# Three-pass embedding in rounded parts, router columns inside other products, and a new order of a turn

## The reference

```python
h = patches @ W.T + b            # 196 patches of 768 pixels -> 192
h = concat([cls, h]) + pos_embed
h = concat([h, txt], axis=1)     # (32, 274, 192)
h = h + attention(layernorm(h))  # 12 heads of 16, rotary q and k, causal
n = layernorm(h)
pc = softmax(n @ Wsc + bsc); pu = softmax(n @ Wsu + bsu)    # two routers, 4 experts each
common = expert[argmax(pc)](n)   # 192 -> 768 -> gelu -> 192
unique = expert_u[argmax(pu)](n) # counts only for tokens past the capacity 2192 of their common expert
out = h + common + dropped * unique
```

## Time and profile before

| | |
|---|---|
| median of 3 runs | 1303.76 us (1300.44 to 1304.24) |
| the profiled execution, own time | 1305.39 us |
| its span, first to last instruction | 1303.5 us |
| mean granted TensorE clock | 0.962 |
| TensorE / VectorE / ScalarE / GpSimd busy | 92% / 68% / 43% / 48% |

### The profile page before, as it was taken

How to read it: one execution, slowest core, us unless ns; L and a number is a source line. 1 busy time by engine, 2 the same in 40 slices (tenths; PEclk the granted TensorE clock), 3 DMA queues, 4 the chain that set the end, 5 groups by cost and what they waited for, 6 DMA issues and landing times.

```text
span 1303.5 us, 33182 instructions
## 1 busy us (share of the span) xinstructions
PE 1202.0 (92%) x12718; PEld 1026.7 (79%) x12718; DVE 883.1 (68%) x1979; ACT 555.9 (43%) x959; POOL 621.8 (48%) x990
## 2 busy tenths in 40 slices
PE   5799999999999999999999999884899999999993
PEld 4667777777777877877787777674899999999993
DVE  5667677777777778678777767745898755554441
ACT  1134434444434443434443444332454555555540
POOL 4133333334543553454444544443552677765665
PEclk8899999999999999999999999885899999999997
DMA  6001121122312322232232222237787688987651
GB/s 204 31 30 42 44 75 45 43 63 84 108 56 61 115 93 58 84 125 62 82 99 89 80 75 67 66 108 271 272 271 253 208 276 270 293 261 255 220 186 32
DMA packets 84367, 168.03 MB, mean 129 GB/s; under 512 B 16446, under 2 KB 57701, under 8 KB 84208
## 3 DMA queue, kind: packets, MB, share of 16 engines
q1 hardware_dynamic: 70544, 139.88, 33.7%
q0 software_dynamic: 13664, 26.00, 5.6%
HBM read 123.83 MB, written 45.45 MB: 130 GB/s over the span
## 4 chain that ended last, share of the span: by engine, by line
PE 46%; DVE 22%; issue 12%; POOL 12%; DMA 3%; ACT 2%; SPq 1%; POOLq 0%; DVEq 0%; ACTq 0%
PE h_ps L1677 10%; PE y_ps L1688 9%; DVE capped L995 4%; POOL sorted_d L235 4%; PE round_banks L591 3%; PE gen L553 3%; PE gen L511 3%; POOL PT L877 3%; DVE xn L1011 3%; PE round_banks L564 3%; PE gen L520 2%; DVE nm L999 2%; DVE nm L997 2%; POOL rstd L870 2%; PE round_banks L578 2%
## 5 line engine op out<-in xcount | busy, mean ns | idle before, releaser
L760 ACT ACTIVATE PT<-round_banks 128x1752 f32<-128x1752 f32 x96 | 156.6, 1631 | 175.4 <-PE round_banks L591 175.4
L877 POOL TENSOR_SCALAR_AFFINE_SELECT PT<-PT 128x512 f32<-128x512 f32 x192 | 117.8, 637 | 206.3 <-ACT PT L760 205.8
L1767 ACT ACTIVATE Gl<-h_ps,W 128x256 f32<-128x256 f32 x264 | 115.8, 474 | 172.1 <-PE h_ps L1677 163.9
L1688 PE MATMUL y_ps<-W,Gl 128*128 128x192 f32 x1056 | 181.2, 325 | 0.0
L1688 PEld LDWEIGHTS y_ps<-W,Gl 128*128 128x128 f32 x1056 | 171.3, 189 | 0.0
L1677 PE MATMUL h_ps<-XH,Wh 128*128 128x256 f32 x528 | 149.0, 299 | 7.0 <-DVE Wl L1834 2.8
L511 PE MATMUL gen<-w_emb,xT 128*128 128x192 f32 (+1 forms) x768 | 143.8, 339 | 7.8 <-DMA ident<-in_ident_dram 7.8
L1677 PE MATMUL h_ps<-XH,Wl 128*128 128x256 f32 x528 | 141.4, 289 | 0.0
L511 PEld LDWEIGHTS gen<-w_emb,xT 128*128 128x128 f32 (+1 forms) x768 | 119.6, 171 | 16.7 <-DMA ident<-in_ident_dram 7.8
L591 PEld LDWEIGHTS round_banks<-QKT 32*128 32x128 f32 x2304 | 95.3, 187 | 46.7 <-DVE nm L997 23.0
L995 DVE TENSOR_TENSOR capped<-round_banks,masks_f 128x1024 f32<-128x1024 f32 x96 | 116.2, 1211 | 17.3 <-PE round_banks L564 16.8
(11 more groups left out here) (273 smaller groups left out, 2448.4 us busy)
## 6 DMA issues: line engine op xcount, KB each, us to landing
W<-in_experts_dram SPq DMA_DIRECT2D x44, 771.0 KB, 5.3
W<-in_experts_dram SPq DMA_DIRECT2D x44, 672.0 KB
xT<-in_xT_dram SPq DMA_DIRECT2D x32, 591.0 KB, 4.4
X<-sorted_d SPq DMA_DIRECT2D x35, 386.0 KB, 6.2
stage<-rows_d SPq DMA_DIRECT2D x64, 192.0 KB
rows_d<-h SPq DMA_DIRECT2D x32, 192.0 KB
out_dram<-h SPq DMA_DIRECT2D x32, 192.0 KB
rows_d<-xn SPq DMA_DIRECT2D x32, 192.0 KB
```

What stands on the lines that cost most here:

```text
L760: act.activation(PT[(JG * b + j) % 2][:], R[:, :, 0:438], ACT.Exp, scale=SCALE).then_inc(exps, 1)
L877: pool.affine_select(x[:, :, at:at + P], x[:, :, at:at + P], [[0, GH], [1, P]], ALU.is_ge, 0.0, base=0, channel_multiplier=-1)
L1688: mm = pe.matmul(y_ps[t.par][:, k * D:(k + 1) * D], Gl[t.par][:, f, k * P:(k + 1) * P], W[t.i][:, W2O + f * D:W2O + (f + 1) * D], start=(f ...
L1767: act.activation(Gl[t.par][:, f, :], h_ps[f % 3][:, 0:ROWS], ACT.Gelu, bias=W[t.i][:, B1O + f:B1O + f + 1]).then_inc(g_ready, 1)
```

## The change

It has four parts.

1. **Embedding in rounded parts.** Pixels x are split into `xh`, rounded to the format fp32r by ScalarE (`round_pixels`), and `xl` = x - `xh` by GpSimd (`rest_of_pixels`); the weights likewise, once at the start. A chunk is then one product of `xh` with both weight parts side by side (384 columns) and one of `xl` with the high part (192 columns). VectorE adds the two halves of the bank. Both splits of image t + 1 stand at the end of turn t on their engines.
2. **Router as extra columns.** The router is linear in h, and h is the embedding plus the attention's output. Eight columns are added to the value weights and to the output weights (`DE` = 200); the part from V is scaled by the standard deviation and kept (`part_logits`), that from WO is added, and the sum is scaled with `rstd2` and given its bias in `soften`. The centred router weights and their product with the output weights are made in turns 0 to 2 with R's banks. X2, RT, X2t and RTt, with their copies, go.
3. **Second normalisation on ScalarE.** `normalise` does scale and shift of `xn2` by one activation per tile; GpSimd makes the shift (`shift`). The tail's stays on VectorE.
4. **New order of a turn.** TensorE: M0, values 1, values 2, X, S0, V0, QK0, M1, E0, V1, S1, QK1, UT0, UT1, M2, E1, AT, T, values 0, KQ0, KQ1, MT, S2, KQ2, WO. VectorE and ScalarE follow; GpSimd's root for LN1 comes behind both rotary additions.

```diff
-STEADY = [("PV1", 4), ("PV2", 4), ("E0", 0), ("X", 1), ("E1", 0), ("V0", 1), ("QK0", 1), ("UT0", 4), ("UT1", 4), ("QK1", 1),
-          ("KQt0", "1"), ("KQt1", "1"), ("X2", 5), ("V1", 1), ("PV0", 3), ("XTt", "0"), ("ATt", "8"), ("RTt", "10"), ("UTt", "7"),
-          ("AT", 4), ("RT", 5), ("RK", "12"), ("QKt", "0"), ("X2t", "9"), ("KQ0", 1), ("KQ1", 1), ("MT", 2), ("Vt", "0"), ("KQ2", 1), ("WO", 4),
-          ("WOt", "8")]
+STEADY = [("PV1", 4), ("PV2", 4), ("X", 1), ("V0", 1), ("QK0", 1), ("E0", 0), ("V1", 1), ("QK1", 1), ("UT0", 4), ("UT1", 4),
+          ("KQt0", "1"), ("KQt1", "1"), ("E1", 0), ("AT", 4), ("XTt", "0"), ("ATt", "8"), ("UTt", "7"), ("PV0", 3),
+          ("QKt", "0"), ("KQ0", 1), ("KQ1", 1), ("RK", "12"), ("MT", 2), ("Vt", "0"), ("KQ2", 1), ("WO", 4), ("WOt", "8")]
...
-        w_emb = sb("w_emb", [P, EC, D])
-        w_qkv = sb("w_qkv", [P, 2, 3 * D])
-        w_o = sb("w_o", [P, 2, D])
+        w_emb = sb("w_emb", [P, EC, 2, D], F32R)
+        w_qkv = sb("w_qkv", [P, 2, 3 * D + NE])
+        w_o = sb("w_o", [P, 2, DE])
         w_r = sb("w_r", [P, 2, NE])
+        r_bias = sb("r_bias", [P, NE])
+        woT = sb("woT", [KC, 2, 2, KC + 1])
         minus_half = sb("minus_half", [P, 2])
 
         xT = [sb(f"xT{i}", [P, EC, NPATCH + 1]) for i in range(2)]
+        xh = sb("xh", [P, EC, NPATCH + 1], F32R)
+        xl = sb("xl", [P, EC, NPATCH + 1], F32R)
...
             def embed(b, k):
                 if k == 0:
-                    pe.wait_ge(x_in[b % 2], 16 * (b // 2 + 1))
+                    if b == 0:
+                        pe.wait_ge(emb_low, 1)
+                    pe.wait_ge(xl_set, b + 1)
                 g = fill(f"E{k}", b)
                 cols, m = (slice(0, P), P) if k == 0 else (slice(P, NPATCH + 1), IMG1)
                 for c in range(EC):
-                    mm = pe.matmul(g[0:m, 0:D], xT[b % 2][:, c, cols], w_emb[:, c, :], start=(c == 0), stop=(c == EC - 1))
+                    if c:
+                        pe.matmul(g[0:m, 0:D], xl[:, c, cols], w_emb[:, c, 0, :], start=False, stop=False, skip_group_check=True)
+                    mm = pe.matmul(g[0:m, 0:2 * D], xh[:, c, cols], w_emb[:, c, :, :].rearrange("p s d -> p (s d)"),
+                                   start=(c == 0), stop=(c == EC - 1), skip_group_check=True)
+                    if c == 0:
+                        pe.matmul(g[0:m, 0:D], xl[:, c, cols], w_emb[:, c, 0, :], start=False, stop=False, skip_group_check=True)
                 filled(f"E{k}", b, mm)
...
-            def route(use, i, xTs, tiles):
-                g = fill(use, i)
-                for k in range(tiles):
-                    o = g[:, k * NE:(k + 1) * NE]
-                    pe.matmul(o, xTs[:, 0, tok(k)], w_r[0:KC + 1, 0, :], start=True, stop=False)
-                    mm = pe.matmul(o, xTs[0:KC, 1, tok(k)], w_r[0:KC, 1, :], start=False, stop=True)
-                filled(use, i, mm)
+            def centre_router():
+
+                pe.wait_ge(consts_set, n_set)
+                pe.matmul(R[0:KC, 0, 0:NE], K.ones[0:KC, 0:KC], w_r[0:KC, 0, :], start=True, stop=False)
+                pe.matmul(R[0:KC, 0, 0:NE], K.ones[0:KC, 0:KC], w_r[0:KC, 1, :], start=False, stop=True).then_inc(mean_filled, 1)
+
+            def turn_output_weights():
+
+                pe.wait_ge(later_in, 16 * len(later))
+                for j in range(2):
+                    for c in range(2):
+                        at = (2 * j + c) * (KC + 1)
+                        mm = pe.transpose(R[0:KC, 1, at:at + KC + 1], w_o[0:KC + 1, c, j * KC:(j + 1) * KC], ident[0:KC + 1, 0:KC + 1])
+                mm.then_inc(wo_turned, 1)
+
+            def mix_output_weights():
+
+                pe.wait_ge(wo_copied, 1)
+                pe.wait_ge(centred, 1)
+                for c in range(2):
+                    o = R[0:KC + 1, 2, c * NE:(c + 1) * NE]
+                    pe.matmul(o, woT[:, 0, c, :], w_qkv[0:KC, 0, 3 * D:3 * D + NE], start=True, stop=False)
+                    mm = pe.matmul(o, woT[:, 1, c, :], w_qkv[0:KC, 1, 3 * D:3 * D + NE], start=False, stop=True)
+                mm.then_inc(wo_mixed, 1)
+                pe.wait_ge(wo_set, 1)
...
+            def round_pixels(b):
+
+                act.wait_ge(x_in[b % 2], 16 * (b // 2 + 1))
+                if b:
+                    act.wait_ge(g_filled[bank("E1", b - 1)], nth("E1", b - 1))
+                act.activation(xh[:], xT[b % 2][:], ACT.Copy).then_inc(xh_set, 1)
+
+            act.wait_ge(first_in, 16 * len(first))
+            act.activation(w_emb[:, :, 0, :], w_raw, ACT.Copy).then_inc(emb_high, 1)
+            round_pixels(0)
             act.wait_ge(consts_set, n_set)
...
             def copy_values(use, i, k):
                 g = take(use, i)
-                emptied(use, i, act.activation(V[i % 4][:, k, :, 0:HD], g[:, 0:D].rearrange("p (h d) -> p h d", d=HD), ACT.Copy))
+                act.activation(V[i % 4][:, k, :, 0:HD], g[:, 0:D].rearrange("p (h d) -> p h d", d=HD), ACT.Copy)
+                act.wait_ge(std_ready, i + 1)
+                emptied(use, i, act.activation(part[:, i % 8, k, :], g[:, D:DE], ACT.Copy, scale=std[:, i % 2, k:k + 1]))
+
+            def normalise(b):
+
+                if b >= 2:
+                    act.wait_ge(rows_out[b % 2], stored(b - 2))
+                act.wait_ge(shift2_ready, b + 1)
+                c = UNIT * (b // 4) + 2 * (b % 4)
+                for k in range(2):
+                    ins = act.activation(xn2[b % 2][:, k, :], h[b % 8][:, k, :], ACT.Identity,
+                                         bias=shift2[:, b % 2, k:k + 1], scale=rstd2[:, c + k:c + k + 1])
+                ins.then_inc(xn2_ready, 1)
...
                     copy_heads(t.pre, 2)
+                if t.t + 1 < B:
+                    round_pixels(t.t + 1)
...
+            def rest_of_pixels(b):
+
+                pool.wait_ge(xh_set, b + 1)
+                if b:
+                    pool.wait_ge(g_filled[bank("E1", b - 1)], nth("E1", b - 1))
+                pool.tensor_tensor(xl[:], xT[b % 2][:], xh[:], ALU.subtract).then_inc(xl_set, 1)
+
             for x in (rr, rrt, nm, *ht, *QKT):
                 pool.memset(x[:], 0.0).then_inc(zeroed, 1)
+            rest_of_pixels(0)
...
+            def shift(b):
+
+                c = UNIT * (b // 4) + 2 * (b % 4)
+                if b:
+                    pool.wait_ge(shift2_ready, b)
+                pool.tensor_scalar(minus[:], mv[:, LN2, :, 0], -1.0, None, ALU.mult).then_inc(minus_ready, 1)
+                pool.wait_ge(rstd_ready[LN2], b + 1)
+                pool.wait_ge(minus_ready, b + 1)
+                if b >= 2:
+                    pool.wait_ge(xn2_ready, b - 1)
+                pool.tensor_tensor(shift2[:, b % 2, :], minus[:], rstd2[:, c:c + 2], ALU.mult).then_inc(shift2_ready, 1)
+
+            def spread(b):
+
+                pool.wait_ge(rstd_ready[LN1], b + 1)
+                if b >= 2:
+                    pool.wait_ge(g_emptied[bank("V1", b - 2)], nth("V1", b - 2))
+                pool.tensor_tensor(std[:, b % 2, :], veps[:, LN1, :], rstd[:, LN1, :], ALU.mult).then_inc(std_ready, 1)
+
+            def spread_tail(g):
+
+                pool.wait_ge(rstd_ready[LN1T], g + 1)
+                pool.tensor_tensor(stdt[:, g:g + 1], veps[:, LN1T, 0:1], rstd[:, LN1T, 0:1], ALU.mult).then_inc(stdt_ready, 1)
...
                 if t.at is not None:
                     causal(t.at, 2)
+                if t.t + 1 < B:
+                    rest_of_pixels(t.t + 1)
                 n = staging(t.t + 1)
                 if n is not None:
                     if n < 2:
@@ -941,6 +1029,7 @@
                     prepare(pool, K, H, n)
                 if t.t % 4 == 3 and (t.t + 1) // 4 < NG:
                     root(LN1T, (t.t + 1) // 4, 1)
+                    spread_tail((t.t + 1) // 4)
...
+                dve.wait_ge(g_emptied[bank("WO", 4 * u + 3)], nth("WO", 4 * u + 3))
+                dve.wait_ge(g_emptied[bank("WOt", u)], nth("WOt", u))
+                dve.wait_ge(rstd_ready[LN2], 4 * u + 4)
+                dve.wait_ge(rstd_ready[LN2T], u + 1)
+                mine = by_token[:, cols(u), :]
+                lg = mine.rearrange("p c (s e) -> p c s e", s=2)
+                then(dve.tensor_tensor(mine, mine, bc(rstd2[:, cols(u)].rearrange("p (c a) -> p c a", a=1), [P, UNIT, NE]), ALU.mult))
+                then(dve.tensor_tensor(mine, mine, bc(r_bias[:].rearrange("p (a e) -> p a e", a=1), [P, UNIT, NE]), ALU.add))
                 then(dve.tensor_reduce(mx[:], lg, AX.X, ALU.max))
...
+            def add_attention(b):
+
+                g = take("WO", b)
+                c = UNIT * (b // 4) + 2 * (b % 4)
+                both = g[:, 0:2 * DE].rearrange("p (k c) -> p k c", c=DE)
+                dve.tensor_tensor(by_token[:, c:c + 2, :], both[:, :, D:DE], part[:, b % 8, :, :], ALU.add)
+                x = h[b % 8][:]
+                emptied("WO", b, dve.tensor_tensor(x, both[:, :, 0:D], x, ALU.add))
+
```

(25 more changed lines are left out.)

307 lines of the change are left out of this document (153 added, 154 removed).

## The result

The changed kernel takes 1329.7 us (median of 4 runs, 1328.1 to 1330.5), the kernel before beside it 1302.6: a ratio of 1.0207, 95% interval 1.0175 to 1.0239. It is some 2% slower, where I forecast 1290 and a range that ended at 1308. The profiled execution took 1329.25 us, span 1327.5.

A forecast was written before the change was run, and what follows sets the result against it. TensorE was taken to bound the attention stage; 57 us saved in steady turns, less 43 for stalls and 4 at the start, plus 3 at the end, gave 1292 profiled and 1290 as median, range 1250 to 1308.

The forecast's parts named there:

- E0: TensorE's embedding of the 128-token half, each turn: 2.15 us before, forecast 1.84; both halves together save 0.85 a turn.
- the stall: S0 in turns 4, 8, ..., 28 waits 5.3 us, as GpSimd's root comes behind the subtraction and holds up M0's reading.
- I take 1.9 lost per pause: Behind each wait of S0, TensorE at half clock for some 3.8 us loses 1.9 us, between 0 and 2.5.
- 4 us lost: Start: E0 waits 5.1 us, turns 1 to 4 save four times 2.1, turn 4 stalls 7.2; between 1 won and 7 lost.
- The weights' round trip: At turn 2, through VectorE; counted in full only in the start's bound of 7 us lost.
- 8.5 us a four: TensorE's saving in four steady turns; turns 5 to 31 are 6.75 such fours, 57 us if waits stay as they are.
- even: VectorE loses two scalings and gains two additions of 192 columns.
- 3 us won: End: turns 32 and 33 still lose X2 and RT; nothing counted in later turns (0 to 6).
- 13 us of clock: The forecast's cost of TensorE's clock falling, which the tidier case took away.
- No stall: Rival: S0's wait is hidden somewhere unseen, 43 + 7 us come back, 1240; chance 0.13.
- The maximum row: Rival: S0 waits for MT's row by DMA; 0.7 us in each of the other 20 turns gives 1304; chance 0.17.
- The subtraction: Slower rival: GpSimd's pixel subtraction far dearer than the 2.8 us taken; at 6 us, 1328; chance 0.10.

The follow-up runs named there:

- the kept-busy kernel: Changed kernel plus six unread products of 384 columns before S0 in each turn with t%4==0 from t=4, the stall left in: 1303.9 us, ratio 1.0017.
- the scaling late: Changed kernel with VectorE's scaling of the next tail (xnt) moved behind the reading of M0 in the turn after: 1268.4 us, ratio 0.9739.
- the kernels with one sum: Changed kernel, scaling moved, tail's divide earlier, unread products at start, embedding summed in the same 192 columns: 1253.5 us for both halves, 1246.0 for the 69-token half.
- kernels with the fp32 embedding: Changed kernel with the unsplit embedding: 1290.3 us; with scaling moved and tail's divide earlier 1265.6; with unread products at the start too 1255.5.
- the start kept busy: Seven unread products in the pauses of turns 2 and 3: 1320.3 us on the changed kernel, 1254.7 with scaling moved and tail's divide earlier.

## Why the prediction was wrong

**The mechanism of the stall was right.** Its place, its cause, the rows of its chain and its length (4.75 us for 5.3) came as worked out. Without that stall the change is a gain; with it I forecast a smaller gain, and it was a loss, because four terms of the sum were mis-sized. Against the 1292 of the sum, the profiled 1329.25 is 37 more:

- **The clock, "I take 1.9 lost per pause": mis-sized.** The earlier trace rows looked behind a pause of 2.08 us that had cost 3.8 us at half speed. Here the clock stayed low for 10 to 14 us, and the loss was 4.6 to 5.5 us, in four of the six steady passages. A fifth, at 310 us, waited only 1.51 us, since TensorE had already been at half clock from 300 to 308, behind MT's wait; at the sixth the kept-busy kernel had a slow stretch of its own (693 to 700), so that they don't differ there, though the changed one loses some 3 us. Sum 20 us (the kernel kept busy against the changed one), counted 11: **+9**. My bound of "between 0 and 2.5" came from one case and was no bound.
- **The start, "4 us lost": mis-sized.** It was 16: **+12**. The half clock behind two pauses of 2.5 and 2.0 us in turns 2 and 3 cost 7 to 9 us, counted nothing: the products in these pauses bring S2 of turn 3 from 89.5 to 82.1 us in the changed kernel, from 91.1 to 82.0 with the scaling late. The weights' round trip stood in my bounds as a wait and not as the start of a slow stretch. Turn 4's stall with its clock cost 9.0, of which 4.3 are the wait (from that S2 to turn 5's addition 36.65 us, 27.64 with the scaling late), counted 7.2. What is left, the late start less what the turns save, came out even, counted 3.3 won. So 10 to 12 of the 12 us are clock.
- **The saving, "8.5 us a four": mis-sized.** It was 6.7. Free of the stall, four turns took 96.8 us and not 95.0, over 6.75 of them **+12**. E0 and E1 saved 0.73 a turn and not 0.85 by their rows, and the kernels with one sum show where the rest of the embedding's part went: I had called VectorE's trade "even" by sums of busy time, but its two extra additions stand in its chain to the maxima and before a bank that TensorE waits for. With one of them gone, four turns take 95.2 for 96.6.
- **The stall itself**: 50.5 us lie between the changed kernel's steady turns and those without it. Less the clock's 20 that leaves 31, counted 32: **-1**.
- **The end, "3 us won"**: turns 32 to 36 took 71.0 us, before 70.0: **+4**. Turn 33 alone is 3.8 longer, and in it the clock stood at 0.51 over 21 us, before at 0.62 over 9. Not all of the +4 is loss: in the traces of the experiments the same turns took 68.0 to 72.6 us, and none of these runs was made for them. The rest, 2 us, lies behind turn 36.

The step that failed is thus the clock's price: "I take 1.9 lost per pause, between 0 and 2.5", and nothing for the pauses of the start. The runs show 4.6 to 5.5 us behind a stall of 4.75, and 7 to 9 at the start. In the steady turns, behind turn 4's stall and at the start it is 19 to 21 of the 37 us, which by itself carries 1292 to 1311 or more and past the range's 1308. The missing saving by itself (1304) would not have left it.

A check on this: the kept-busy kernel less what the start's products gave, 1303.9 - 9.4 = 1294.5, is an estimate of the changed kernel with its stalls and nearly without the half clock (the two were not run together). My sum without its 13 us of clock would be 1277. The 17 between them are the saving, the end and the rest. That 1294.5 lies near my 1290 is chance: there the missing saving stands in for the clock that I did count.

**The rivals.** "No stall" came only by another edit. The maximum row never took over S0: in no steady turn does S0 wait for a transfer. The subtraction was no dearer than its proportion (2.71 us in the median). The slower rival I had named was thus the wrong one; the true one, a long low clock behind my own predicted stall, I had priced and closed.

**Left open.** No run moved the first product alone (13.68 for 7.75 us). The kernels with the fp32 embedding, whose first product comes at 7.4 us, reach turn 5's addition no sooner than their like (120.0 for 118.7, and 115.1 for 109.6 with the start kept busy), so it cost little; but their clock in the first turns differs too. Nor did a run show what makes one pause of 1.5 to 1.9 us cost clock and another not. The router's columns and the second normalisation on ScalarE were never undone by themselves.

## What to carry to other kernels

When a step is put into an engine's queue, list what stands behind it and who waits for that; moving the one small root (0.6 us) or its reader was worth 50 to 60 us, more than the change's whole saving. Price a pause of the bound engine with the slow stretch behind it, from the row with the worst case and not from one mild one, and count the pauses at the start too. Extra work on an engine that is not the bound is free only where it isn't in a chain the bound engine waits on; test it there, not by its busy share.

## What the runs showed of the hardware

- After a pause of 4.75 us TensorE ran at 1.2 GHz for over 9 us though it had work without a gap; behind the other stalls of that length the low clock lasted 7 to 14 us. Pauses of 1.9 us brought either the low clock (3.2 us lost) or nothing, in one and the same program, and a wait of 1.5 us brought 3 to 7 us of it once in each of four traces. I had expected some 1.9 us lost for a pause of either length.
- Unread products in a pause kept the clock at 1.00 behind it: six of them per stall took 26 us off the whole, seven at the start 9.4.
- For the same 576 columns in three one-pass products, six chunks took 2.09 us with 128 columns of weights to load each time and 1.66 with 69; with two loads a chunk 1.82 and 1.63.
- GpSimd's two-input subtraction of 1182 columns into the rounded format took 2.71 us, 2.3 ns a column, and 3.59 the first time, at the start.
